# Two weight sums moved to VectorE with places of their own, other sums and the gates placed later, and eight tiles of W1 prepared in the second span

## The reference, cut to what matters

```python
# x: (8, 256, 1024); W (1024, 1024); Wr (8, 1024); A (8, 16, 1024); B (8, 1024, 16); weight (16, 1024, 1024)
def _L0_cond_ref(x, language_ids, W, Wr, A, B):
    base = jnp.einsum('btd,od->bto', x, W)
    logits = jnp.einsum('btd,ed->bte', x, Wr) + bias[:, None, :]      # bias: 5.0 for the row's own id
    topw, topi = jax.lax.top_k(logits, 2)
    gates = jnp.sum(jax.nn.one_hot(topi, E) * jax.nn.softmax(topw, axis=-1)[..., None], axis=-2)
    h = jnp.einsum('btd,erd->bter', x, A)
    return base + 2.0 * jnp.einsum('bter,bte,eor->bto', h, gates, B)
x = x + _L0_cond_ref(x, itok_B_0_7, L0_cond_W, L0_cond_Wr, L0_cond_A, L0_cond_B)
x = x + jnp.einsum('bsi,boi->bso', x, weight[itok_B_0_15])            # one 1024x1024 matrix for each of 8 rows
```

## Time and profile before

| | us |
|---|---|
| median of 3 runs | 457.25 (456.57 to 457.74) |
| the profiled execution | 460.07 |
| its span, first to last instruction | 458.3 |
| TensorE busy in the span | 408.2 |
| VectorE busy | 317.6 |
| GpSimd busy | 92.0 |

### The profile page before, as it was taken

One profiled execution on the slowest core, in us unless ns is written; L12 is line 12 of the kernel. 1 busy time (PEld: TensorE's weight loads), 2 busy tenths in 40 slices (PEclk: granted clock), 3 DMA queues, 4 the chain that ended last, 5 costly groups with the idle time before them and its releaser, 6 DMA issues.

```text
span 458.3 us, 5994 instructions
## 1 busy us (share of the span) xinstructions
PE 408.2 (89%) x1920; PEld 341.1 (74%) x1920; DVE 317.6 (69%) x400; ACT 167.6 (37%) x239; POOL 92.0 (20%) x108
## 2 busy tenths in 40 slices
PE   8999619799999989999999279947999897999996
PEld 8989517688889878888888267836878685888885
DVE  3899899996627588395831696977778778876900
ACT  2342122746303242534521254353444253443511
POOL 0145786000000730000000123112211321112100
PEclk9999958999999999999999769986999998899999
DMA  8974320123386740026598999999999999999821
GB/s 187 221 212 134 107 63 0 46 93 127 148 192 222 237 85 1 1 92 185 196 307 257 237 284 249 262 282 304 294 327 296 319 285 316 296 316 285 235 70 46
DMA packets 94065, 89.57 MB, mean 195 GB/s; under 512 B 7218, under 2 KB 85586, under 8 KB 94034
## 3 DMA queue, kind: packets, MB, share of 16 engines
q1 hardware_dynamic: 60288, 63.99, 50.7%
q10 hardware_dynamic: 33746, 25.21, 20.2%
HBM read 64.00 MB, written 25.17 MB: 195 GB/s over the span
## 4 chain that ended last, share of the span: by engine, by line
PE 31%; DMA 25%; DVE 17%; SPq 10%; issue 7%; POOL 4%; ACT 2%; ACTq 2%; DVEq 0%; POOLq 0%
SPq L359 10%; DMA raw<-in_L_cond_weight_dram 9%; DMA x_kept<-stage 6%; PE banks L1213 5%; PE banks L1215 5%; PE banks L1214 5%; DMA tokens<-x_kept 5%; PE banks L1116 5%; PE banks L1117 5%; PE banks L1118 5%; DMA ring_f<-in_L_cond_weight_dram 3%; DVE stage L631 2%; DVE weights_f L641 2%; DVE tokens_f L514 2%; DMA raw<-in_x_dram 2%
## 5 line engine op out<-in xcount | busy, mean ns | idle before, releaser
L1213 PE MATMUL banks<-weights,tokens 128*128 128x512 f32 x176 | 72.5, 412 | 23.7 <-DMA tokens<-x_kept 12.6
L1116 PE MATMUL banks<-ring,weights 128*128 128x512 f32 x192 | 76.0, 396 | 14.6 <-DVE weights L528 13.4
L641 DVE STREAM_TRANSPOSE weights_f<-raw 128x1024 f32<-128x1024 f32 x42 | 52.0, 1240 | 36.3 <-POOL raw L444 36.1
L1214 PE MATMUL banks<-weights,tokens 128*128 128x512 f32 x176 | 71.6, 407 | 0.0
L1215 PE MATMUL banks<-weights,tokens 128*128 128x512 f32 x176 | 71.3, 405 | 0.0
L444 POOL TENSOR_TENSOR raw<-raw,ident 128x128 f32<-128x128 f32 x50 | 29.8, 597 | 201.3 <-DMA raw<-in_L_cond_weight_dram 180.2
L958 ACT ACTIVATE weights<-weights_f 128x1024 fp32r<-128x1024 f32 x44 | 45.7, 1057 | 58.7 <-DVE weights_f L641 29.3
L647 DVE TENSOR_TENSOR weights<-weights_f,weights 128x1024 fp32r<-128x1024 f32 x44 | 52.7, 1198 | 13.9 <-ACT weights L958 13.7
L1213 PEld LDWEIGHTS banks<-weights,tokens 128*128 128x128 f32 x176 | 35.1, 199 | 32.8 <-DMA tokens<-x_kept 13.9
L1116 PEld LDWEIGHTS banks<-ring,weights 128*128 128x128 f32 x192 | 36.6, 190 | 23.0 <-DVE weights L528 13.8
L1118 PE MATMUL banks<-ring,turned_w 128*128 128x512 f32 x128 | 49.8, 389 | 0.0
(11 more groups left out here) (106 smaller groups left out, 669.2 us busy)
## 6 DMA issues: line engine op xcount, KB each, us to landing
raw<-in_L_cond_weight_dram SPq DMA_DIRECT2D x168, 128.0 KB, 8.7
x_kept<-stage SPq DMA_DIRECT2D x32, 512.0 KB, 3.5
tokens<-x_kept ACTq DMA_DIRECT2D x16, 1024.0 KB, 15.3
ring_f<-in_L_cond_weight_dram SPq DMA_DIRECT2D x88, 128.0 KB, 8.6
raw<-in_x_dram SPq DMA_DIRECT2D x64, 128.0 KB, 3.2
out_dram<-sums ACTq DMA_DIRECT2D x32, 256.0 KB, 8.9
raw<-in_L_cond_W_dram SPq DMA_DIRECT2D x32, 128.0 KB, 2.8
raw<-in_L_cond_A_dram SPq DMA_DIRECT2D x4, 128.0 KB, 3.0
```

The source lines that it names most:

```text
L641: nc.vector.transpose(w1_turn(n).rearrange("p (m q s) -> p q m s", m=M, q=Q), raw_tile(SLOT[item]).rearrange("p (q m j) -> p q m j", q=Q, ...
L1116: nc.tensor.matmul(ps, u_hi, x_hi, start=first and k == 0, stop=False, skip_group_check=True)
L1213: nc.tensor.matmul(l1_bank(o), x_hi, w_hi, start=m == 0, stop=False)
L1214: nc.tensor.matmul(l1_bank(o), x_hi, w_lo, start=False, stop=False)
```

## The change

`sums2`, a buffer of TensorE's sums that is free until product 6 is copied, now holds S2, and the place of product 4's weights (`4h`) now holds T2 of the first span. S3 and S2 run on VectorE. T4 of the first span, S4 and the difference for B run on GpSimd, behind T3. On VectorE the four `add_p1` and the gates come behind the low parts of product 7 and of B. On TensorE `turn_gated` comes behind three quarters of product 7, and `lora` 11 behind all of it. In the second span VectorE prepares eight of W1's tiles, with four turns ahead of `add_up(1, "11", r)`, and nine tiles use the three raw slots. ScalarE's list stands two tiles further ahead in the second layer.

```diff
-    EARLY = 6
+    EARLY = 9
+    EARLY_TURNS = 8
...
-        SLOT["w1", n] = (N_LOADS + n) % RAW if n < EARLY else (n - EARLY) % RAW1
+        SLOT["w1", n] = (N_LOADS + n) % RAW if n < EARLY else (n - EARLY + RAW) % RAW1
...
         def s2_sum(r):
-            at = op_at("6l") + r * HALF
-            return weights_f[:, at:at + HALF]
+            return sums2[:, r]
+
+        t2_early = weights_f[:, op_at("4h"):op_at("4h") + OP].rearrange("p (m f) -> p m f", m=HM)
...
-            for n in range(RAW):
+            for n in range(5):
                 load_w1(n)
             keep_all(1, "11")
-            load_w1(3)
-            load_w1(4)
+            load_w1(5)
+            load_w1(6)
+            load_w1(7)
             keep_all(1, "22")
-            load_w1(5)
+            load_w1(8)
             keep_all(1, "21")
-            for n in range(EARLY, EARLY + RAW):
-                load_w1(n)
             load_w1(9)
+            load_w1(10)
             keep(1, "12", 0)
             keep(1, "12", 1)
-            load_w1(10)
+            load_w1(11)
             keep(1, "12", 2)
-            load_w1(11)
+            load_w1(12)
...
             for r in range(HM):
                 add_ones(("w", HM + r))
-                make_s3(r)
-                make_s2(r)
+            pool.wait_ge(s2_done, HM)
             for t in range(XT):
                 make_t3(0, t)
             for r in range(HM):
+                make_s4(r)
+            sum_bd()
+            for r in range(HM):
                 make_s1(r)
+            for t in range(XT):
+                make_t4(t)
...
                 if s:
                     turn_w1(0)
                     turn_w1(1)
+                    low_w1(0)
+                    turn_w1(2)
+                    low_w1(1)
+                    turn_w1(3)
                 for r in range(HM):
                     add_up(s, "11", r)
...
             for o in range(L1_OUTS):
-                for n in range(M + 2 * o, M + 2 * o + 2):
+                for n in range(M + 2 + 2 * o, M + 2 + 2 * o + 2):
                     if n < NW1:
                         high_w1(n)
                 put_out(o)
...
                 product(s, 6, lambda r: pe.wait_ge(p1_copied, HM * s + r + 1), False, main_bank)
+                product(s, 7, lambda r: pe.wait_ge(u2_copied, HM * s + r + 1), False, main_bank, range(HM - 1))
                 turn_gated(s)
-                product(s, 7, lambda r: pe.wait_ge(u2_copied, HM * s + r + 1), False, main_bank, range(HM - 1))
+                product(s, 7, None, False, main_bank, range(HM - 1, HM))
                 pe.wait_ge(gT_done, s + 1)
...
                     lora(s, "11", r)
-                product(s, 7, None, False, main_bank, range(HM - 1, HM))
```

More of the change, by code:

```diff
@@ L680, in _ @@
             make_t2(0, 0)
[L681 removed]
             turn(x_item(0, 1, 2))
+            low(("x", 0, 6, 0))
             make_t2(0, 1)
[L684 to L685 removed]
             turn(x_item(0, 1, 3))
+            low(("x", 0, 6, 1))
             make_t2(0, 2)
[L688 to L689 removed]
             turn(("w", 4))
+            low(("x", 0, 6, 2))
             make_t2(0, 3)
[L692 to L693 removed]
+            make_s3(0)
+            make_s2(0)
             turn(("w", 5))
             low(("x", 0, 6, 3))
[L696 removed]
+            make_s3(1)
+            make_s2(1)
+            low(("u", 6, 0))
             turn(("w", 6))
[L698 to L700 removed]
+            make_s3(2)
+            make_s2(2)
+            low(("u", 6, 1))
             turn(("w", 7))
[L702 to L704 removed]
+            make_s3(3)
+            make_s2(3)
             low(("u", 6, 2))
[L706 removed]
             low(("u", 6, 3))
[L708 to L709 removed]
             lows("u", 7)
[L711 to L712 removed]
+            turn(("b",))
+            lows("x", 0, 7)
+            low(("b",))
+            for r in range(HM):
+                add_p1(0, r)
             dve.wait_ge(setup, 4)
             make_gates(0)
[L715 to L718 removed]
             gT_low(0)
[L720 removed]
             low(("bd",))
@@ L818, in _ @@
             x1_low(1, "12", 1)
-            turn_w1(7)
-            low_w1(6)
             turn_w1(8)
-            low_w1(7)
+            turn_w1(9)
+            low_w1(8)
             x1_low(1, "12", 2)
             x1_low(1, "12", 3)
-            for n in range(9, NW1):
+            for n in range(10, NW1):
                 turn_w1(n)
@@ L1009, in span @@
                 highs("x", s, 5)
+                if s:
+                    for n in range(3):
+                        high_w1(n)
                 x1_high(s, "11", 0)
@@ L1038, in span @@
                 if s:
-                    high_w1(3)
+                    high_w1(4)
+                    load_x1(0)
+                    high_w1(5)
                 x1_high(s, "21", 0)
```

162 lines of the change are left out of this document (64 added, 98 removed).

## The result

The changed kernel takes 464.3 us (median of 4 runs, 460.61 to 467.25), and the kernel before, run beside it, 457.5 us (456.57 to 458.43): ratio 1.013, with 95% between 1.009 and 1.017. The change makes the kernel some 6 us slower. The forecast was 456.7 us with a range up to 462.5, so it was wrong, and the range did not hold the time.

The account below looks back on a forecast made before the run. TensorE's waits were taken as the bound, then full transfers (296 GB/s), then the clock. Terms -4.3 - 1.2 + 10.7 - 5.8 = -0.6 us took the median from 457.25 to 456.7 us, range 451.5 to 462.5.

Parts of the forecast that it names:

- Product 6 (A): First span: TensorE's wait ahead of product 6 falls from 13.41 to 2.1 us, without the clock's fall: -13.4 us.
- The gates (B): First span: TensorE waits 8.2 us (bounds 0 and 15) ahead of the gates' turns; A and B together -4.3 us.
- Rival G: First span: GpSimd ends its sums by 75, B's wait is 3 us or less; total 451.7 us; chance 0.19, another rival included.
- C: Second span: the gates go behind product 2's low parts and the 1.21 us wait goes: -1.2 us.
- The turn of tile 3 (D): Second span: tile 3's turn holds TensorE 8.1 us ahead of product 5, plus 2.6 for the clock: +10.7 us.
- The second layer (E): Second layer: 5.3 us from three more landed tiles and 0.5 for the shorter end: -5.8 us (bounds -2 and -9).
- rival F: Second layer keeps little, since later rows' loads wait for later tiles: E is -2, time 460.5 us; chance 0.26.
- The offset: Whole kernel: the 2.8 us between profiled execution and median was taken as the same in both kernels.
- Rival H: Second layer: the removed 11.08 us wait carries through, E is -9, time 453.5 us; chance 0.15.

Follow-up runs that it names:

- after_again: The changed kernel once more, unaltered, against the kernel before: 465.42 us (6 runs), ratio 1.0128.
- b_lead: The kernel before with only ScalarE's list two tiles further ahead in the second layer: 464.32 us, ratio 1.0111.
- a_nolead: The changed kernel with ScalarE's list in the second layer as it was, without the two tiles' lead: 459.45 us, ratio 1.0021 to the kernel before.
- e_late: The changed kernel with W1's turns of the second span moved behind product 4's tokens: 461.25 us, ratio 1.0032 to the kernel before.
- e_nolead: e_late without ScalarE's lead of two tiles: 455.58 us, ratio 0.9928 to the kernel before.
- e_best: e_nolead with row loads ahead of the high parts and the first layer's result kept by row and partition: 449.96 us, ratio 0.9775 to the kernel before.
- n_xfirst: a_nolead with the load of the row after next ahead of the high parts: 456.99 us, ratio 0.9976 to the kernel before.
- f_xrows: n_xfirst with the first layer's result kept by row and partition, in 8 KB pieces: 452.47 us, ratio 0.9887 to the kernel before.

## Why the prediction was wrong, step by step

**Product 6 (A)** was right. It starts at 56.02 behind 2.39 us, against 55.8 and 2.1, and the half clock behind the old wait is gone: the granted clock is 1.00 from 56 to 60 us, where the kernel before had 0.50 from 67 to 69.5.

**The gates (B)** were right: the turns start at 82.90 behind 7.58 us (forecast 83.1 and 8.2), at half clock (granted 0.50 from 82.9 to 89 us; 1.97 us in place of 1.09), and product 5 at 93.35 behind 1.03 us (92.9, 1.0). The bound from 0 to 15 us was wide, and the choice near its middle, with VectorE and GpSimd taking turns, held: the gates took 7.5 us (75.33 to 82.85), where 5.3 and 2.4 were counted. In after_again the wait is 5.95 us, since TensorE came there 1.1 us later, but the turns start at 82.33 all the same. Rival G was wrong.

**C** was right: no wait stands there in the profile after.

**The turn of tile 3 (D)** was right in its time: 7.50 us against 8.1, and GpSimd's ones release the turn. SyncE's load, GpSimd's ones and VectorE's turn:

```profile
198.93 4.17 SPq L362 DMA_DIRECT2D raw<-in_L_cond_weight_dram  x8
...
203.09 0.80 POOL L447 TENSOR_TENSOR raw<-raw,ident 128x128 f32<-128x128 f32 x1 [39.86 <-DMA raw<-in_L_cond_weight_dram]
...
203.92 1.25 DVE L650 STREAM_TRANSPOSE weights_f<-raw 128x1024 f32<-128x1024 f32 x1 [0.35 <-POOL raw L447]
```

One detail was off: VectorE was to stand idle for about 3 us ahead of this turn and stood 0.35 us, because the low parts of tiles 0 and 1 and the turn of tile 2 fill the time. Without the wait for the load product 5 would have begun 0.35 us sooner.

The second layer starts at 249.61, forecast 249.5. In after_again it starts at 248.07.

**The second layer (E)** failed. In the first profiled execution it seemed to hold: 205.1 us from first to last matmul, in place of 209.9, and 204 forecast. In after_again the same kernel took 211.7. Of the 6.7 us between the two, 2.9 are there when row 1 begins (the wait is 7.33 us in place of 4.44), and 5.1 when row 6 begins. The transfers moved 296 and 292 GB/s from 280 to 410 us, which is 0.5 MB or 2 us. At row 6 the wait is 3.58 us in place of 1.62, and the granted clock falls behind it (0.52 from 414.7 to 416.7), where it stayed at 1.00 in the first execution:

```profile
277.32 0.76 PE L1213 MATMUL banks<-turned_w,tokens 128*128 128x512 f32 x1 [7.33 <-issue]
...
414.77 0.80 PE L1213 MATMUL banks<-weights,tokens 128*128 128x512 f32 x1 [3.58 <-DMA tokens<-x_kept]
```

The step that failed is a term that the sum of E put at nothing. The sum counts 5.3 us of lead in bytes and 0.5 for the shorter end. "ScalarE's two further tiles ahead of each output" stand in it only among the new waits that "take the rest" of the wait that was removed; they cost nothing of the 5.8. b_lead puts their price at 1.1%, 5 us. The mechanism was in the text as rival F and in E's bound of -2, with 3.5 us named for it, and then weighed down by "three tiles of lead". The two are one account: tiles that run ahead are a gain only if what TensorE waits for is tiles. From row 2 on it waited for rows, and a tile ahead of a row's load is a loss. Without the lead the sum of -0.6 us comes nearly out: a_nolead measured +1.0, with an interval from -0.6 to 2.6.

That this much came out is in part luck. The sum added what moves the layer's start (-5.5 for A to C, +10.7 for D) to a length that did not depend on the start. The runs show that it does: e_late starts 8 us sooner than the changed kernel and is 4.2 us faster, e_nolead against a_nolead 9 and 3.9. So about half of a later start comes back as a shorter layer, and the split between the start's +5.2 and E's -5.8 is not borne out, only their total.

F's own test, the landing of tile 17, was met in favour of the forecast: GpSimd had it at 286.77, 37.2 us into the layer, where F was to begin at 38. It was no test of the row's load, which left at 291.66.

**The offset** failed too, without a part in the miss of the median. The forecast took the 2.8 us between the profiled execution and the median for something that both kernels have. It is the draw of one execution: the profiled one of the kernel before lies 1.3 us above the median of 29 runs, that of the changed kernel 3.7 us below its median of four. So it is luck that the sum for the profiled executions, 459.5 against 460.61, was close. Between the medians the change was to give -0.6 us and gave +6.8 (by the ratio +5.9, from 4.1 to 7.8). About 5 of that are the lead; the rest is no larger than the interval is wide, and stays open.

**Rival H** (the removed 11.08 us carry through) was wrong: 9.9 of them come back ahead of rows 1 and 2, where 4.4 and 14.8 us stand in place of 0.9 and 8.4. Ahead of row 1 it is a wait for a tile still, and 7.3 us in after_again, 9.1 in e_late and 9.9 in e_nolead.

What stays open is why the first profiled execution got off so lightly, beyond its transfers' rate, and how the 9.5 us between a_nolead and e_best divide between bytes and order.

## What to carry to other kernels

Where transfers bind, count the bytes that stand ahead of each load, and ask of each whether the engine at the end waits for it: running further ahead with one stream delays the other by its bytes at the bound rate. A start that comes sooner was worth about half its length here, and the bytes that moved in it would account for that, so look at the stretch where the transfers are not yet full. Size a term from several executions where it hangs on waits for transfers, and keep the distance between one execution and the median as a width, not as an offset.

## What the runs showed of the hardware

Stores ran beside loads for nothing: with 0.79 MB fewer stored per row the pace of rows stayed 24.7 us, and the rate fell from 296 to 266 GB/s with the DMA share unchanged at 1.12 to 1.13. With loads cut by 1.05 MB per row the kernel fell by 17.6 us. So a DMA share over 1 and a sum in GB/s did not tell what was bound here; the loads' own rate did, 256 GB/s, and 251 with the sixth cut.

Pieces of 8 KB in place of 1 KB for a third of the loads' bytes shortened their landing from 14.9 to 10.5 us and left the pace at 24.7 (n_xfirst) and 24.8 us (f_xrows) per row.

The Trainium skill, in "DMA: Bandwidth & Descriptors", section "Bandwidth", gives 341 GB/s for a load of 1 MB and 425 GB/s for one of 16 MB, issued from GpSimd on 128 partitions. The stretch where loads bind here stays below that: the two queues of SyncE and ScalarE, with transfers of 128 KB and 1 MB beside the stores, gave 256 GB/s of loads, and 296 with the stores. For this kernel the measured rate is the one to size with.
